# Forty early tiles of any expert, the last group's chain written between the tiles of the second part

## What is computed

```python
# graph layer: B=8, N=1024, D=128, H=512
agg = epsilon * ln(x) + einsum('bnm,bmd->bnd', adjacency, ln(x))
h   = silu(rmsnorm(agg @ W1 + b1) * rms_weight)
x   = x + h @ W2 + b2
# experts: E=8, the two best of each token
xn  = layernorm(x)
topk_scores, topk_idx = top_k(xn @ Wg.T + bg, 2)
combine = sum(softmax(topk_scores)[..., None] * one_hot(topk_idx, 8), -2)
for e in range(8):
    y   = relu(xn @ W1[e].T + b1[e]) @ W2[e].T + b2[e]
    out = out + combine[..., e:e+1] * y
x   = x + out
```

## Time and profile before

| what | value |
|---|---|
| median of three executions | 596.34 us |
| the profiled execution | 599.59 us, its span 597.6 us |
| granted PE clock, mean over the span | 0.973 of full |
| PE busy | 546.7 us (91%) |
| POOL busy | 408.9 us (68%) |
| DVE busy / ACT busy | 353.6 us (59%) / 291.7 us (49%) |
| row scatters, line 886 | 128, mean 1033 ns |
| result scatters, line 955 | 142, mean 976 ns |

### The profile page before, as it was taken

The page is one execution under the profiler, slowest core; times in us unless marked ns, Lnnn a source line. Parts: engine busy times, 40 slices in busy tenths (PEclk is TensorE's granted clock), DMA queues, the critical chain, the costliest instruction groups (busy, mean ns, idle before and its releaser), DMA issues.

```text
span 597.6 us, 13049 instructions
## 1 busy us (share of the span) xinstructions
PE 546.7 (91%) x3704; PEld 452.7 (76%) x3704; DVE 353.6 (59%) x1174; ACT 291.7 (49%) x779; POOL 408.9 (68%) x664
## 2 busy tenths in 40 slices
PE   1999999999999999999598899999999999999872
PEld 0466765677666676667497899999999999999840
DVE  2457696877958779577546544444445445444463
ACT  3355655555474454754343455455455455455411
POOL 5223788787886869877557887666776766767550
PEclk9999999999989989999878999999999999999995
DMA  8998333454424444231025777666667666666798
GB/s 368 321 398 335 105 122 146 173 172 169 158 68 147 168 171 152 96 126 33 18 89 214 254 274 263 248 237 255 252 238 261 252 238 254 248 248 248 251 412 329
DMA packets 40518, 127.18 MB, mean 213 GB/s; under 512 B 7775, under 2 KB 19808, under 8 KB 38272
## 3 DMA queue, kind: packets, MB, share of 16 engines
q1 hardware_dynamic: 31232, 108.88, 49.6%
q0 software_dynamic: 8640, 16.93, 8.4%
q10 hardware_dynamic: 576, 0.53, 0.3%
HBM read 61.19 MB, written 24.02 MB: 143 GB/s over the span
## 4 chain that ended last, share of the span: by engine, by line
PE 54%; POOL 17%; DMA 8%; issue 8%; DVE 5%; ACT 5%; SPq 3%; POOLq 0%; ACTq 0%; DVEq 0%
POOL slots L886 9%; PE ps_y L653 9%; PE ps_g L653 8%; PE ps_agg L545 7%; PE ps_y L529 6%; POOL x_all L879 3%; DMA slots<-rows,dest 3%; PE ps_agg L640 2%; PE ps_agg L639 2%; PE ps_t L628 2%; ACT hn L702 2%; PE ps_h L639 2%; PE ps_agg L643 2%; PE ps_h L643 2%; PE ps_h L640 2%
## 5 line engine op out<-in xcount | busy, mean ns | idle before, releaser
L955 POOL DMA_INDIRECT parts<-adj_in x142 | 138.6, 976 | 68.7 <-ACT adj_in L798 51.6
L886 POOL DMA_INDIRECT slots<-rows,dest x128 | 132.2, 1033 | 23.4 <-issue 23.2
L545 PE MATMUL ps_agg<-adj_in,xn_both 128*128 128x512 f32 x256 | 128.8, 611 | 12.9 <-ACT xn_both L693 12.9
L798 ACT ACTIVATE adj_in<-adj_in,share 128x128 f32<-128x128 f32 x142 | 49.4, 395 | 117.3 <-issue 105.0
L1219 DVE TENSOR_TENSOR xe_split<-ps_t,xe_split 128x256 fp32r<-128x256 f32 x71 | 30.1, 425 | 73.4 <-ACT xe_split L780 72.0
L545 PEld LDWEIGHTS ps_agg<-adj_in,xn_both 128*128 128x128 f32 x256 | 45.6, 197 | 36.7 <-issue 34.1
L653 PE MATMUL ps_y<-W2e,hb 128*128 x576 | 70.2, 275 | 0.4 <-issue 0.4
L653 PE MATMUL ps_g<-W2e,hn 128*128 x560 | 68.1, 275 | 0.0
L653 PEld LDWEIGHTS ps_y<-W2e,hb 128*128 128x128 f32 x576 | 67.3, 192 | 0.6 <-issue 0.6
L529 PEld LDWEIGHTS ps_y<-consts,siluT 128*128 128x128 f32 x512 | 60.7, 192 | 7.2 <-issue 7.2
L653 PEld LDWEIGHTS ps_g<-W2e,hn 128*128 128x128 f32 x560 | 65.4, 191 | 0.0
(11 more groups left out here) (179 smaller groups left out, 1153.7 us busy)
## 6 DMA issues: line engine op xcount, KB each, us to landing
wcur<-expert_w SPq DMA_DIRECT2D x71, 578.0 KB, 3.5
adj_in<-in_adjT SPq DMA_DIRECT2D x16, 2048.0 KB, 8.4
adj_in<-slots SPq DMA_DIRECT2D x71, 130.0 KB
expert_w<-parts SPq DMA_DIRECT2D x8, 512.0 KB, 10.6
out<-x_all SPq DMA_DIRECT2D x8, 512.0 KB, 6.6
x_all<-in_x SPq DMA_DIRECT2D x1, 3072.0 KB, 23.6
parts<-adj_in POOLq DMA_INDIRECT x142
expert_w<-in_F1T SPq DMA_DIRECT2D x1, 2048.0 KB, 18.6
```

The lines of the kernel that those rows point to most:

```text
L545: ins = pe.matmul(ps_agg[par][:, :], xn[b % 2][:, m, :], adj_in[par][:, m, :], start=(m == 0), stop=(m == TPB - 1))
L798: ins = act.activation(ye[ku][:, j, :], yb[ku % 2][:, j, :], ACT.Copy, scale=share[ku][:, j:j + 1])
L886: pool.indirect_dma_start(out=slots, out_offset=bass.IndirectOffsetOnAxis(ap=dest[q % 2][:, c, j:j + 1], axis=0), in_=rows[q % 2][:, c, j, ...
L955: pool.indirect_dma_start(out=parts, out_offset=bass.IndirectOffsetOnAxis(ap=goes[u % 8][:, j, :], axis=0), in_=ye[ku][:, j, :], in_offset ...
```

## The change

`EARLY` becomes 40: the full tiles (256 rows of one expert, any expert) that the first 12 groups hold. DVE counts them in step 14 (`full_tiles`, `early_tiles`) and writes a 40-row table, from which SP and PE read each early tile's row and expert. Tiles 0 and 1 are transposed inside the second layer of group 14. The chain of groups 14 and 15 after the last group step is cut up, and its pieces stand between the pieces of tiles 0 to 19. `keep_busy` is gone. The silu of group 15 becomes a sigmoid on ACT and a product on DVE, so that ACT's table is loaded once, ahead of the tiles. Until tile 20 (`BOTH_PAIRS`) the PSUM banks `ps_t1` and `ps_g` serve the chain, and the tiles use `ps_t0` and `ps_y` alone. The rows of group 14 are scattered in the steps 7, 9, ... 21 of POOL, one of eight in each, and those of group 15 in the steps 24, 26, ... 38. SP's four paddings now stand ahead of its load of tile 36, ACT's in the steps 20 to 23. The buffers `slot` move to `adj_in0`, and `hT`, `ye` and `yb` to `adj_in1`.

```diff
-    EARLY = 2 * GTOK * (NG - 2) // E // TILE
+    GE = 12
+    EARLY = (2 * GTOK * GE - E * (TILE - 1)) // TILE
+    BOTH_PAIRS = 20
...
@@ SP
-                        sp.wait_ge(s_scat[i], 16 * GT * (NG - 2))
-                    sp.wait_ge(s_mm, NG)
+                        sp.wait_ge(s_scat[i], 16 * 2 * GT * ((GE + 1 - i) // 2))
+                    sp.wait_ge(s_mm, NG - 1)
                 elif t == EARLY:
                     for i in range(2):
                         sp.wait_ge(s_scat[i], 16 * GT * NG)
                     sp.wait_ge(s_pads, 16 * (SPARE + E))
...
-            sp.wait_ge(s_tail, 1)
-            fill_tails(sp, range(0, E // 2))
...
+                if t == EARLY - 4:
+                    sp.wait_ge(s_tail, 1)
+                    fill_tails(sp, range(0, E // 2))
@@ PE, in step 15, and after the last step
+                if g == NG - 1:
+                    pe.wait_ge(s_silu, 4 * g)
+                    for t in range(2):
+                        transpose_rows(t, t)
                 if has(g, 1):
                     second_layer(g - 1, (2, 3))
...
-            first_layer(q, range(GT))
-            transpose_normed(q - 1, ps_y)
-            gate(q - 1)
-            keep_busy(ps_agg[0], 20)
...
+            pe.wait_ge(s_x1, last)
+            pe.wait_ge(s_base, last - 1)
+            first_layer(last, range(GT), (ps_h[0], ps_h[1], ps_y, ps_g))
@@ PE, tile(t, k), after the first layer of tile t-1
+                if t == 3:
+                    transpose_normed(last - 1, spare_bank)
+                elif t == 4:
+                    pe.wait_ge(s_hb, 4 * last + 4)
+                    gate(last - 1)
+                    pe.wait_ge(s_hn, NG)
+                    pe.wait_ge(s_hna, NG)
+                    transpose_hidden(last, (0,), [spare_bank] * HC)
...
+                elif t == 12:
+                    transpose_normed(last, spare_bank)
+                elif t == 13:
+                    gate(last)
+                elif t == 15:
+                    rank(last)
                 if live(t, 2):
...
-                    wait(pe, s_yb, u - 1)
+                    wait(pe, s_yb, u if u <= BOTH_PAIRS else u - 1)
+                    bank_ = ps_g if u > BOTH_PAIRS and u % 2 else ps_y
@@ POOL, scatter_results(t, k), after the two results of tile t-2
+                if 7 <= t < 23 and t % 2:
+                    if t == 7:
+                        pool.wait_ge(s_dest, last)
+                        pool.wait_ge(s_row2, last)
+                    c, j = place_of_scatter((t - 7) // 2)
+                    scatter_rows(last - 1, c, (j,))
+                elif t == 10:
+                    ln2_factors(last)
+                elif 22 < t < 39 and t % 2 == 0:
...
+                    c, j = place_of_scatter((t - 24) // 2)
+                    scatter_rows(last, c, (j,))
@@ DVE, step 14
+                if g == GE + 2:
+                    full_tiles()
                 if has(g, 1):
                     scale_hidden(g - 1)
                 if has(g, 2):
                     first_choice(g - 2)
                     second_choice(g - 2)
+                if g == GE + 2:
+                    early_tiles()
@@ DVE, tile(t, k), after yb of tile t-2
+                elif t == 8:
+                    ln2_stats(last)
+                    ln2_aggregate(last)
+                elif t == 11:
+                    normed_rows(last)
+                elif t == 13:
+                    first_choice(last)
+                elif t == 14:
+                    second_choice(last)
+                elif t == 15:
+                    last_places()
```

More of the change, by code:

```diff
@@ L1088, in step @@
             def step(g, par, b):
-                order.step((g + 1) * 22)
+                order.step((g + 1) * 40)
                 if has(g, 2):
@@ L1128, in step @@
                     places(g - 2)
-                if has(g, 1):
+                if has(g, 1) and g < NG - 1:
                     add_second_layer(g - 1)
@@ L1166, in _, with low_of_rows @@
-            first_choice(q)
-            order.end()
-            def last_choice():
-                order.step((NG + 3) * 22)
-                second_choice(NG - 1)
+            last = NG - 1
+            spare_bank = ps_t[1]
+            order.step((NG + 1) * 40)
+            def low_of_rows(t, k):
+                bank_ = ps_t[1] if t % 2 and (t == 1 or t >= BOTH_PAIRS) else ps_t[0]
+                dve.wait_ge(s_eTh, t + 1)
+                dve.tensor_tensor(xeT_lo[k % 2], bank_[:, 0:TILE], xeT_hi[k % 2].bitcast(FP32),
+                                  ALU.subtract).then_inc(s_eTc, 1)
```

386 lines of the change are left out of this document (208 added, 178 removed).

## The result

| what | before | after |
|---|---|---|
| median of 20 executions each | 596.91 us | 599.99 us |
| ratio, with its 95% interval | | 1.0054 (1.0036 to 1.0073) |
| the profiled execution, its span | 597.6 us | 598.5 us |
| granted PE clock, mean over the span | 0.973 | 0.983 |

The kernel became slower by 3.1 us, 0.5%, where 3.6 us less were forecast. In size it is within the 1% that was called no change, but the interval leaves out 1.000, the sign is not the forecast one, and 600.0 us lies above the range (587.5 to 598.5).

What follows compares the result with a forecast made beforehand. PE was taken as the bound in the tiles, with idle and constant work between the parts. Saving 24.4 us less 20.8 of new losses gave 3.6 us saved: a median of 592.7 us, range 587.5 to 598.5.

Steps and rivals of the forecast that it cites:

- step 14 and 15, DVE: DVE's counting of full tiles and the table make normalised rows and scale factors reach PE late: 0.45 us lost.
- the first steps: Steps up to 7: PE waits for DVE's addition, ACT's relus and small misfits: 2.4 us lost, from 1.5 to 5.
- step 12: PE waits for group 15's normalised rows, whose root stands behind tile 8's scatters: 2.3 us and 0.2 more.
- steps 14 and 15, the rank: The rank waits for `second_choice` in steps 14 and 15: 0.5 us lost.
- tile 36: SP's four paddings delay the load of tile 36's rows: 4.0 us of PE wait, from 3 to 4.9.
- tile 40: SP's load of tile 40 waits for the last row scatter to land: 7.45 us of PE wait, from 6.5 to 9.
- The clock: Half clock after PE's waits: 2.5 us for tile 40, 1.0 for tile 36 and step 12; 3.5 together, from 1 to 6.
- The addition of group 14's second layer: PE waits about 0.75 us for DVE's addition, because group 15's first layer needs bank `ps_y`.
- A: Rival: the new waits are shorter, every term at its lower end; 10.3 us saved, 586.0 us; chance 0.20.
- B: Rival: tiles 36 and 40 don't wait, loads run four tiles ahead; 18.3 us saved, 578.0 us; chance 0.06.
- C: Rival: POOL falls behind in steps 24 to 38; kernel slower, 604.1 us at 1.66 us a scatter; chance 0.08.
- D: Rival: shared banks up to tile 20 cost 0.3 us in each of 20 steps; 6 us lost, 598.7 us; chance 0.06.

Runs made afterwards that it cites:

- e12: e8 with PE's wait for DVE's addition of group 14's second layer moved ahead of the third block of group 15's first layer; 581.77 us, ratio 0.9758.
- e1: Changed kernel with PE's read of a tile's expert moved from right before its second layer to the start of the step; 594.73 us, ratio 0.9985.
- e6: Changed kernel with BOTH_PAIRS at 16 instead of 20, so second layers from tile 17 on may use either bank; 599.91 us, ratio 1.0056.
- e8: Changed kernel with expert read and group 15's root earlier, its row scatters in steps 23 to 30, SP's paddings one at a time; 581.05 us, ratio 0.9728.
- e5: Changed kernel with 56 identity transposes on PE right before it waits for tile 40's rows; 596.9 us, ratio 1.0011.
- e2: Changed kernel with group 15's eight row scatters in steps 23 to 30, one in each, instead of 24, 26, ... 38; 590.12 us, ratio 0.9885.
- e4: Changed kernel with POOL's factors for group 15's second normalisation ahead of tile 8's two result scatters, instead of behind; 597.38 us, ratio 1.0017.
- e9: Kernel before with PE's read of a tile's expert moved to the start of the step, on the slow chip; 645.01 us, ratio 1.0233.
- e10: The same kernel as e12, run on the chip of e9; 636.63 us, ratio 1.0117.

## Why the prediction was wrong, step by step

The mechanisms on SP's and POOL's queues were right, and the sum failed in terms that were too small. I compare by the ruler; "measured" is the changed kernel against the kernel in which the wait is gone.

| term | forecast | measured | from |
|---|---|---|---|
| step 14 and 15, DVE | 0.45 | 1.2 | the second half of group 14's second layer begins 27.20 us behind the wait at 259.38 (at 286.58), before 25.51 behind the one at 261.56; less 0.47 for T |
| the first steps | 2.4 | 4.9 | 1.07 (e12), 2.65 (e1), and waits of 0.55 and 0.65 that are left in e12 |
| step 12 | 2.5 | 3.2 | e6, 11.72, less e8's 8.55 |
| steps 14 and 15, the rank | 0.5 | 1.8 | 1.47 (e1), and 0.33 left |
| tiles 22 to 28 | 0 | 1.2 | 21.69 less six steps |
| tile 36 | 4.0 | 2.8 | its wait |
| tile 40 | 7.45 | 6.5 | e5 less e8 |
| the clock | 3.5 | 6.0 | 1.6 (changed less e6, 12 to 14), 1.8 (tile 36: 4.61 less its wait), 2.6 (e5) |
| sum | 20.8 | 27.6 | |

27.6 - 24.4 is 3.2 us slower. Tile 70's wait and what follows its transpose, left at nothing in the forecast, gave back 0.7 (0.76 for 1.49) and 0.5 us (35.7 for 36.2); 2.0 us are left, and 3.1 measured. About half of the 1.1 us between them is in the 24.4. An estimate from e8: its 257.4 us (next paragraph), less 2.7 us of waits up to step 15, less the 4.9 us that it takes from 22 to 35 over the limit, less 0.8 at tile 70, are 249.0; before, the stretch took 274.3 less 1.5 at tile 70, 272.8. That makes 23.8 us to save, not 24.4. Half a us stays unaccounted for, which is within what the medians can tell.

**What bounds the kernel, what goes.** Right in kind: between the parts and up to tile 8 PE's idle and constant work is gone, and e8 shows 257.38 us from behind step 15's T to tile 70's, of which PE is busy 250.4; before, this stretch took 274.3 (287.07 to 561.34).

**The first steps: the step that failed most.** The prediction counted DVE's and ACT's work beside each piece of PE's, and no instruction of PE's own. The changed order had L606 in it, a read that PE didn't do before for the first seven tiles (`early_expert` was read once) and that was hidden for the others. With it 2.65 us are lost in steps 3 to 6 and 1.47 in step 15, and the forecast of the loss had to be 4.1 us higher: more than the forecast gain. The rule that each instruction of a moved step counts was kept for SP's reads of the table and not for PE's.

**The addition of group 14's second layer** was foreseen as a wait (0.75 us, measured 0.83), and e12 shows that it cost 1.09.

**Step 12.** Place and releaser were right: 2.86 us on DVE's `rows` where 2.3 and 0.2 were said.

**Tile 36.** Right in kind, too large in size: 2.83 us of 4.0, just below the lower end of 3. SP's four paddings took 4.10 us, the rows went out at 432.60 and were used 2.19 us later; the forecast allowed up to 3.5 for that.

**Tile 40.** Right in every link but one landing time. The row scatter was said to start 4.84 us after the end of L2 of tile 36, which is where T of tile 39 begins, and starts 5.00 after it. It landed in 2.34 us (2.32 to 2.34 in the six other kernels with this wait), not 3.57, and that is why 6.23 us and not 7.45 were waited. The rule of the Trainium skill (DMA: Bandwidth & Descriptors, "Anatomy of one DMA") that the prediction set against the row, an estimated 2.15 us for such a scatter, was nearer here than the row that I stayed with. What differs is the load on the DMA engines meanwhile (last two numbers: their share, GB/s), first before during the scatter of the earlier trace rows, then in the changed kernel:

```profile
337.30:341.20 3.90, 3.90 (x36) 3.90 (x36) 1.85 (x5) 2.42 (x9) 3.53 (x6) 1.00 0.66 241
```

```profile
451.70:454.00 2.30, 0.00 (x0) 0.00 (x0) 0.00 (x0) 0.00 (x0) 2.13 (x3) 1.00 0.17 57
```

With PE and SP standing still the engines were nearly free, and I had taken a landing time from a stretch in which they were two thirds busy. That this is the cause was not tested.

**The clock.** The mechanism was right and its size was not. I gave two of the three places 1.0 us together, since waits of 1.39 and 1.49 us had left the clock at full. Waits of 2.8 us did not here: 1.6 and 1.8 us. With how it falls in other profiles (none in step 12 in e2 and e6, 3.0 us at tile 36 in e6) the 6.0 us are what this one execution paid and not a fixed price.

**The rivals.** A, B and C are out: no wait was shorter than its lower end except by 0.2 us at 36 and 0.3 at tile 40; both tiles waited; the scatters kept their 0.98 and 1.03 us. The rule of the Trainium skill (GPSIMD Engine Reference, "1. Specifications") on the SBUF interfaces that POOL shares with VectorE again showed nothing here: DVE's added work changed neither mean by more than 0.01 us. D is out by e6 as a cost of its own. The case that came true, all places about as forecast and a cost on PE's own sequencer, was none of them. A range that ended at D's 598.5 had no such case above it.

## What to carry over

When a step gets other pieces put into it, list what the waiting engine's own sequencer does between two of its instructions (register reads for an address, above all) and move it ahead of the first wait of the step: 0.9 us here are free there and cost 1.4 behind a wait. A wait for a shared bank ahead of the read takes from the read's lead too: here it started 0.87 us ahead of L2 with it, and 1.4 to 1.95 without. Price a wait of 2.8 us or more on PE with another 0 to 3 us for the clock (1.6, 1.8 and 2.6 in the changed kernel's profile). And when work is spread out so that it fits beside the tiles, ask for its last piece's due time: eight scatters, one in every second step, were 6 us late where the same eight in a row cost 0.2 us, and the idea of the change is worth 16 us (581.05 us) once four such places are mended.

## What the runs showed of the hardware

- **A register read by PE's sequencer** took 0.30 to 0.95 us (1.30 once, at tile 70), with 0.15 us of register arithmetic behind it, and in step 15 began only when the wait ahead of it was over (358.8, the rank having started at 358.63). The Trainium skill (Perfetto Trace Analysis, "Sequencer Loop") says that engine instructions are put in a queue and wait for their semaphores there, while control instructions are started by the sequencer. By this the read could have run during the rank's wait. The row shows that it did not. Nor was it held by the waits for relus and `yb` that stand between the two: the last of these, DVE's `yb`, had ended at 357.13.
- **The clock's fall is not the same in each execution.** The same wait of 2.86 us in step 12 was followed by 0.50 in the changed kernel and by full clock in e6 and in e2 (2.83 us); e4's two gaps of 0.38 and 1.41 us in step 15 were followed by 0.52 and e2's 0.33 and 1.39 by 0.50, and the changed kernel's 0.33 and 1.39 were not. The time of such a stretch changes by up to 1.6 us from one profile to the next with the same code in it, which is why edits were judged by stretches and medians together.
- **One chip ran all three kernels tried on it 40 to 55 us slower** (637.7 us for the kernel before, 645.0 for e9, 636.6 for e10). In e10's profile there the second layers have gaps inside a run of 16 matmuls that nothing in the profile explains. This was not looked into.
